# Conditional residual kernel: the adapters' first weights loaded before the ids are known, the order of its first turns changed

## The reference

```
x = x + einsum('bct,bcd->bdt', x, cond_weights[cond])        # per sample 64 x 64
x = x + einsum('bsi,boi->bso', x, adapter_weight[adapter])   # per sample 1024 x 1024
cond    = randint(0, 16, (128,));  adapter = randint(3, 8, (128,))
```

## Time and profile before

| | |
|---|---|
| median of three runs | 795.91 us |
| profiled execution | 799.4 us |
| its span, first to last instruction | 797.7 us |
| PE busy | 780.7 us, 98% |
| granted clock, mean | 0.997 |
| first z matmul starts | 24.88 us |
| slot 1 starts | 36.79 us |
| last PE work ends, by the chain of waits | 792.70 us |

### The profile page before, as it was taken

The page is one execution under the profiler, slowest core; times in us unless marked ns, Lnnn a source line. Parts: engine busy times, 40 slices in busy tenths (PEclk is TensorE's granted clock), DMA queues, the critical chain, the costliest instruction groups (busy, mean ns, idle before and its releaser), DMA issues.

```text
span 797.7 us, 19299 instructions
## 1 busy us (share of the span) xinstructions
PE 780.7 (98%) x3480; PEld 646.8 (81%) x3481; DVE 590.1 (74%) x707; ACT 455.9 (57%) x773; POOL 254.5 (32%) x158
## 2 busy tenths in 40 slices
PE   5999999999999999999999999999999999999997
PEld 4788888888888888888888888888888888888885
DVE  7777987788887567888876788887576756756764
ACT  3565666566556555765655566566554654555554
POOL 1444434243452212335431243452122122122110
PEclk9999999999999999999999999999999999999998
DMA  8345454444532334444333444532332233233133
GB/s 249 98 110 153 128 144 122 124 123 138 154 99 85 105 91 119 128 148 139 98 105 105 121 121 141 156 97 88 105 96 76 78 105 91 67 105 102 60 102 81
DMA packets 73956, 90.91 MB, mean 114 GB/s; under 512 B 13781, under 2 KB 64470, under 8 KB 73942
## 3 DMA queue, kind: packets, MB, share of 16 engines
q1 hardware_dynamic: 63654, 58.11, 24.2%
q10 hardware_dynamic: 10288, 32.65, 14.4%
HBM read 57.15 MB, written 33.55 MB: 114 GB/s over the span
## 4 chain that ended last, share of the span: by engine, by line
PE 97%; DMA 2%; DVE 0%; POOL 0%; issue 0%; SPq 0%; ACT 0%; POOLq 0%
PE z_ps L557 15%; PE z_ps L558 15%; PE first_ps L557 15%; PE first_ps L558 15%; PE z_ps L560 15%; PE first_ps L560 13%; PE y_ps L570 7%; DMA w_nat<-in_L_cond_weight_dram 2%; PE y_ps L538 0%; PE first_ps L538 0%; PE first_ps L641 0%; PE first_ps L639 0%; PE first_ps L638 0%; PE y_ps L652 0%; POOL w_nat L312 0%
## 5 line engine op out<-in xcount | busy, mean ns | idle before, releaser
L353 POOL TENSOR_TENSOR xt_lo<-x_turned,xt_hi 128x1024 fp32r<-128x1024 f32 x61 | 146.6, 2403 | 250.5 <-ACT xt_hi L699 246.5
L557 PE MATMUL z_ps<-w_hi,xt_hi 128*128 (+1 forms) x528 | 205.8, 390 | 0.0
L558 PE MATMUL z_ps<-w_lo,xt_hi 128*128 (+1 forms) x528 | 205.4, 389 | 0.0
L557 PE MATMUL first_ps<-w_hi,xt_hi 128*128 x520 | 202.4, 389 | 0.0
L558 PE MATMUL first_ps<-w_lo,xt_hi 128*128 x520 | 202.3, 389 | 0.0
L560 PE MATMUL z_ps<-w_hi,xt_lo 128*128 (+1 forms) x512 | 199.2, 389 | 0.0
L1005 DVE TENSOR_TENSOR y<-y_ps,y 64x512 f32<-64x512 f32 x252 | 173.2, 689 | 31.9 <-ACT y L715 26.0
L560 PE MATMUL first_ps<-w_hi,xt_lo 128*128 x472 | 183.6, 389 | 0.0
L715 ACT ACTIVATE y<-y_ps 64x512 f32<-64x512 f32 x252 | 149.1, 593 | 9.9 <-issue 2.0
L704 ACT ACTIVATE z_parts<-z_ps 64x512 fp32r<-64x512 f32 x132 | 78.4, 594 | 130.2 <-PE y_ps L570 92.8
L704 ACT ACTIVATE z_parts<-first_ps 64x512 fp32r<-64x512 f32 x130 | 77.2, 594 | 129.4 <-PE y_ps L570 102.8
(11 more groups left out here) (147 smaller groups left out, 387.6 us busy)
## 6 DMA issues: line engine op xcount, KB each, us to landing
x_in<-in_x_dram SPq DMA_DIRECT2D x536, 64.0 KB, 2.6
out_dram<-y ACTq DMA_DIRECT2D x124, 256.0 KB, 3.7
w_nat<-in_L_cond_weight_dram SPq DMA_DIRECT2D x128, 128.0 KB
w_nat<-in_L_cond_weight_dram SPq DMA_DIRECT2D x4, 512.0 KB, 8.1
y<-in_L_cond_weight_dram SPq DMA_DIRECT2D x2, 512.0 KB, 9.3
w_turned<-in_L_cond_weights_dram SPq DMA_DIRECT2D x2, 256.0 KB, 3.9
x_in<-in_x_dram SPq DMA_DIRECT2D x2, 256.0 KB, 5.6
x_turned<-in_L_cond_weight_dram SPq DMA_DIRECT2D x1, 512.0 KB, 6.9
```

The lines of the kernel that those rows point to most:

```text
L353: nc.gpsimd.tensor_tensor(xt_lo[h][:], x_turned[h][:], xt_hi[h][:].bitcast(F32), ALU.subtract).then_inc(xt_lo_made, 1)
L557: nc.tensor.matmul(to, xt_hi[h][:, t, :], whi, start=(t == 0), stop=False)
L558: mm = nc.tensor.matmul(to, xt_hi[h][:, t, :], wlo, start=False, stop=last and not pair)
```

## The change

1. Ids are reversed (7 - id) when the groups are sorted, so the group of id 7 comes first and the group of id 3 last. Its first five chunks are loaded before any id is known; if the first group is not id 7, they are loaded again.
2. The ids are no longer loaded one per partition; two small matmuls spread the clipped rows (`ids_spread`). PE runs 12 matmuls of 128x128 before them and 2 after, whose result nobody reads (`warm`).
3. Turn order: chunks 0 to 3, x of slot 0, chunks 4 to 7 (before: chunks 0, 1, x, 2 to 7). x of slot 0 is loaded with the samples' channels on alternate partitions. Two turns (chunks 6, 7) stand amid z's first half, after 3 and after 5 of its 8 tiles.
4. DVE's remainders are put between the table's small operations; the number of samples in slot 0 is known from the row of ids.
5. The condition matrices are loaded after the chunks. x of slot 1 is loaded half by SP and half by ACT, ACT between its rounding of chunk 6 and chunk 7. DVE turns x of slot 1 before it writes `slot_row`, and waits for `w0_lo_made` before that writing. SP reads `pair_count` after the first chunk load instead of before.
6. At the end, the wait for the store of y's buffer 1 moves behind the placing of W0.

```diff
-        TURN_ORDER = [0, 1, X0, 2, 3, 4, 5, 6, 7]
+        AHEAD_OF_IDS = 5
+        TURN_ORDER = [0, 1, 2, 3, X0, 4, 5, 6, 7]
-        LAST_TURNS = 1
-        TILES_FIRST = 3
+        WARMING, WARMING_ON = 12, 2
+        TURNS_WITHIN = (3, 5)
...
+            for c in range(AHEAD_OF_IDS):
+                sp.dma_start(first_nat[c], adapter_rows[((NAD - 1) * CHUNKS_PER_GROUP + c) * P:((NAD - 1) * CHUNKS_PER_GROUP + c + 1) * P, :]).then_inc(first_loaded[c], 16)
...
+            with sp.If(first_ad < NAD - 1):
+                for c in range(AHEAD_OF_IDS):
+                    sp.wait_ge(first_loaded[c], 16)
+                    load_first(c)
+            with sp.Else():
+
+                for c in range(AHEAD_OF_IDS):
+                    sp.sem_inc(first_loaded[c], 16)
+
+            sp.wait_ge(samples_made, 2)
...
+                sp.dma_start(x_in[0][k:P:2, :], x_rows[bass.ds(sample * C, C), :]).then_inc(x0_loaded, 16)
...
-            sp.wait_ge(table_moved, 16)
-            pairs_past = look_pairs_past(sp)
-            sp.wait_ge(table_ready, 1)
-            sp.wait_ge(groups_ready, 1)
-            sp.wait_ge(first_turned, NH * len(TURN_ORDER))
-            load_chunks(0)
-            load_chunks(1)
+            load_samples([look_early(sp, 2, field) for field in (SAMPLE_A, SAMPLE_B)], 0)
+
+            sp.wait_ge(first_turned, NH * len(TURN_ORDER))
+            sp.wait_ge(groups_ready, 1)
+            sp.wait_ge(table_ready, 1)
+            up_to, = look(sp, 1, CHUNKS)
+            load_chunks_between(0, up_to)
+            pairs_past = look_pairs_past(sp)
             slot(0, 1)
...
+            def warm(times):
+
+                for _ in range(times):
+                    nc.tensor.matmul(first_banks[2][0][:, 0:P], ones, ones, start=True, stop=True)
+
+            pe.wait_ge(consts_made, 3)
+            warm(WARMING)
             pe.wait_ge(consts_made, CONSTS)
+            pe.wait_ge(row_clipped, 1)
+            nc.tensor.matmul(ids_ps[:, 0:1], clipped_row, ones[0:1, 0:1], start=True, stop=True)
+            pe.wait_ge(row_clipped, 2)
+            nc.tensor.matmul(ids_ps[:, 1:2], cond_row, ones[0:1, 0:1], start=True, stop=True).then_inc(ids_spread, 1)
+            warm(WARMING_ON)
             pe.wait_ge(dve_step, MEMBER_STEP)
...
-            turn_first(0)
+            for i in range(TURNS + 1):
+                turn_first(i)
             pe.wait_ge(hot_made, 1)
...
-            for i in range(len(TURN_ORDER)):
+            for i in range(len(TURN_ORDER) - 1):
                 keep_first_hi(i)
+
+            act.wait_ge(table_made, 1)
+            load_sample(act, look_early(act, 1, SAMPLE_B), 1, 1)
+            keep_first_hi(len(TURN_ORDER) - 1)
             act.wait_ge(w0_with_1, 1)
             nc.scalar.activation(w0_all[:, :, 0], w0_nat, ACT.Copy).then_inc(w0_hi_made, 1)
             act.sem_inc(xt_hi_made, 1)
+            keep_z_hi(0, 0, 0)
             keep_xt_hi(1, 1)
-            keep_z_hi(0, 0, 0)
...
-            row_link(nc.vector.tensor_copy(ids_row, ids_row_i))
+            row_link(nc.vector.tensor_scalar(ids_row, ids_row_i, -1.0, float(NAD - 1), ALU.mult, ALU.add))
...
+            turn_x(0, 1)
+
+            dve.wait_ge(w0_lo_made, 1)
 
             dve.wait_ge(table_moved, 16)
...
             dve.wait_ge(table_ready, 1)
-            turn_x(0, 1)
-
-            dve.wait_ge(w0_lo_made, 1)
             turn_chunks(0)
```

More of the change, by code:

```diff
@@ L412, in _ @@
-            for c in range(2):
-                load_first(c)
-            sp.wait_ge(samples_made, 1)
-            _, first_samples = nc.values_load_multi_w_load_instructions(
-                first_samples_i[:], engines=[sp.engine], min_val=0, max_val=B - 1,
-                skip_runtime_bounds_check_because="the table is made on the chip, of clipped indices")
-            for k, sample in enumerate(first_samples):
-                sp.dma_start(x_in[0][k * C:(k + 1) * C, :], x_rows[bass.ds(sample * C, C), :]).then_inc(x0_loaded, 16)
@@ L421, in _ @@
-            for c in range(2, CHUNKS_PER_GROUP):
-                load_first(c)
-            sp.wait_ge(table_made, 1)
-            sp.dma_start(slot_row[:, 1:LOOKED_UP + 1, :], table_i[0:LOOKED_UP]).then_inc(table_moved, 16)
             def load_x(s, h):
                 load_samples(look(sp, s, SAMPLE_A, SAMPLE_B), h)
-            def load_early_x(s, h):
-                _, samples = nc.values_load_multi_w_load_instructions(
-                    table_i[s:s + 1, SAMPLE_A:SAMPLE_B + 1], engines=[sp.engine], min_val=0, max_val=B - 1,
-                    skip_runtime_bounds_check_because="the table is made on the chip, of clipped indices")
-                load_samples(samples, h)
@@ L446, in load_chunks, with load_chunks_between @@
             def load_chunks(s):
-                first, last = look(sp, s, CHUNKS_BEFORE, CHUNKS)
+                load_chunks_between(*look(sp, s, CHUNKS_BEFORE, CHUNKS))
+            def load_chunks_between(first, last):
                 with sp.If(last > first):
@@ L600, in _ @@
             nc.tensor.matmul(seconds_ps, hot[1], vals[:], start=True, stop=True).then_inc(gathered, 1)
[L602 removed]
+            for i in range(TURNS + 1, len(TURN_ORDER) - len(TURNS_WITHIN)):
                 turn_first(i)
[L605 removed]
+            pe.wait_ge(samples_made, 2)
             stores = look_first_stores(pe)
@@ L672, in _ @@
         def _(act):
-            with nc.allow_non_contiguous_dma(reason="one index per partition"):
-                act.dma_start(ids_i[:, 0:1], adapter_ids.rearrange("(b u) -> b u", u=1)).then_inc(ids_loaded, 16)
-                act.dma_start(ids_i[:, 1:2], cond_ids.rearrange("(b u) -> b u", u=1)).then_inc(ids_loaded, 16)
+            act.dma_start(cond_row_i, cond_ids.rearrange("(u b) -> u b", u=1)).then_inc(cond_row_loaded, 16)
             act.wait_ge(consts_made, CONSTS)
@@ L886, in _, with keep_x0_lo, keep @@
             row_linked()
-            nc.vector.tensor_scalar(first_samples_i[:], places[:], 2.0 * B, None, ALU.add).then_inc(samples_made, 1)
+            nc.vector.tensor_scalar(first_samples_i[:, 0:2], places[:], 2.0 * B, None, ALU.add).then_inc(samples_made, 1)
+            def keep_x0_lo(i):
+                def keep(samples, to):
+                    for n in range(NH):
+                        tiles = slice(n * TPB, (n + 1) * TPB)
+                        dve.wait_ge(first_hi_made, NH * i + n + 1)
+                        nc.vector.tensor_tensor(by_sample(to, tiles)[:, :, :, samples],
+                                                in_turns(first_banks[i % TURNS][n][:])[:, :, :, samples],
+                                                by_sample(xt_hi[0], tiles)[:, :, :, samples].bitcast(F32),
+                                                ALU.subtract).then_inc(first_lo_made, 1)
+                dve.wait_ge(samples_made, 2)
+                stores = look_first_stores(dve)
+                with dve.If(stores > 1):
+                    keep(slice(0, 2), xt_lo[0])
+                with dve.Else():
+                    keep(slice(1, 2), xt_hi[0])
             dve.wait_ge(counted, 1)
```

222 lines of the change are left out of this document (128 added, 94 removed).

## The result

The changed kernel takes 799.84 us (median of 6 runs, 798.55 to 800.18), the kernel before 795.89 beside it (795.38 to 796.55): a ratio of 1.0045, 95% interval 1.0035 to 1.0055. It is 3.95 us slower, and outside the forecast's range by 0.6 us. The profiled execution took 800.15 us with a span of 798.4, 0.3 us above its own median; that of before was 3.5 us above its median.

The account below looks back on a forecast made before the run. PE, busy 98% of the span, was taken to bound the kernel. SP's chunk clock leaves 0.15 us of the head's gain, the end costs 0.8: 795.91 + 0.65 = 796.6 us, range 793.6 to 799.2.

Parts of the forecast that it names:

- The head's steps: Head: z at 20.1 us, 4.8 earlier; `table_ready` at 31.8, 1.2 later; slot 1 at 35.0 against 36.79.
- The two stalls of PE: Head: PE stalls 1.6 us ahead of z's other half, waiting for chunk 7's remainder, then waits ahead of slot 1.
- The strided split of x: Slot 0, ACT and DVE: 0.645 at the least, taken; at most twice that, 1.3 us more before z.
- The first step that failed: Method: differences worked out within the profiled execution (799.4 us), then taken off the median, 795.91.
- The second step that failed: Last slot: one sample saves PE 3.63 us; its second half ends by ACT's and DVE's chain, so 1.81 are lost.
- The give-back of 1.0 at the end: End: one matmul fewer, PE starts at once, last store issued sooner with less ahead; 0.3 to 1.7 us together.
- SP's clock: Slot 4: chunk loads follow SP's issues; chunk 3 comes 1.05 us late of 1.2 spare, leaving 0.15 us gain.
- rival A: First group: SP's issues run quicker and do not bind, so slot 1's 1.8 us stay: 794.9; chance 0.17.
- Rival B: Head: ACT's issues hidden or short, table comes with the chunks, PE's work alone counts: 792.4 us; chance 0.13.
- Rival C: Head: PE loses its clock, ids or turns come late, Z at about 22: 798.5 us; chance 0.25.
- Z over 21: Rival C's mark: start of z (Z) later than 21 us; the forecast had 20.1.
- The swizzle: Load of x of slot 0: alternate partitions reach all ports, saving about 1 us of load, none of the sum.

Follow-up runs that it names:

- e_ascending: Changed kernel with ids and groups in ascending order again (early loads take adapter 3), table values clamped at zero: 797.54 us, 1.0017 of before.
- c_before: Control: the kernel before with only a clamp at zero on table values that engines read: 797.16 us, 1.0010 of before.
- e_reversed: Kernel before with only the groups reversed (7 - id), table values clamped at zero: 798.75 us, 1.0031 of before.
- c_after: Control: the changed kernel with only a clamp at zero on table values that engines read: 800.74 us, 1.0054 of before.
- v_best: Changed kernel, ascending, x of slot 0 consecutive, idle matmuls only in two waits, slot 1's x remainder before the table, ACT's reads before its loop: 794.97 us, 0.9986.
- e_end_reads: Changed kernel with ACT's table reads for the last slots moved ahead of its loop, table values clamped: 799.45 us, 1.0032 of before.
- v_reversed: v_best with ids and groups reversed as in the changed kernel: 797.06 us, 1.0010 of before.
- v_no_fill: v_best without its 2 and 4 idle matmuls in the waits: 795.68 us, 0.9994 of before.
- c_after_again: Changed kernel with only the clamp on table values, run and profiled once more: 800.65 us, 1.0054 of before.
- e_x_rows: Changed kernel with x of slot 0 on consecutive partitions, table values clamped: 800.61 us, 1.0054 of before; in a second run 799.87, 1.0048.
- e_nowarm: Changed kernel without its idle matmuls (0 and 0 in place of 12 and 2), table values clamped: 800.62 us, 1.0046 of before.
- e_xt_first: Changed kernel with POOL making slot 1's remainder of x before waiting for the table, table values clamped: 799.98 us, 1.0044 of before.
- e_fill: Changed kernel with x of slot 0 on consecutive partitions and 5 and 4 idle matmuls in two PE waits, table values clamped: 799.02 us, 1.0041 of before.
- e_spec_before: Kernel before with early loads of five chunks (adapter 3), condition matrices' loads moved behind the chunks, table values clamped: 799.11 us, 1.0036 of before.

## Why the prediction was wrong

**The head's steps held.** z at 20.1 (19.95), `table_ready` at 31.8 (31.33), slot 1 at 35.0 (35.52), SP's first chunk at 33.7 (34.12), chunk 7 behind ACT's issues: all within 0.6 us. The two stalls of PE did not: 1.6 us was forecast ahead of z's other half and came as 0.5; 0.75 ahead of slot 1, and came as 1.7. Their sum is right by luck. The strided split of x, taken at its lower bound, cost about two thirds of the way to its upper one: 2.1 us a pair instead of 1.1 on ACT.

Two steps failed, each by about 1.7 us. The numbers for each are worked out from single profiles, so they are estimates.

**The first step that failed: "I work differences out within the profiled execution and take them off 795.91".** The profiled execution was 3.5 us above the median, and the excess sat in the stretch that the change rewrites: slot 1 at 36.79, where an execution nearer the median has 33.4. A changed head that starts slot 1 at 35.5 is 1.3 us early against the one and 2 us late against the other. Before's head waits for its chunk loads, whose landing varies: between 15 us and z PE waited for 1.8, 1.7 and 0 us in its three profiles. The changed one waits for its own chain: 35.52, 35.71, 35.69. In time this shows as follows. e_ascending at its median (797.54) starts the last slot at 776.89. c_before's two profiles, moved to their medians, start it at 775.4 and 775.3. So the new head, with the slots behind it, loses 1.5 us, where the sum had a gain of 0.15. Against the profiled execution the forecast was 799.4 + 0.65 = 800.05, and the changed kernel's profiled execution took 800.15; even that is two errors which cancel, slot 1 early by 1.3 us instead of 0.15 and the rest longer by 2.0 instead of 0.8.

**The second step that failed: in the end's 0.8 us (0.1 to 1.5), that half of the one-sample slot's saving is kept, "1.81 of the 3.63 us are lost".** Nearly all of it was lost. From the start of the last slot to PE's last y row:

| | two samples last | one sample last |
|---|---|---|
| before, c_before; e_reversed | 14.56, 14.64 us | 14.53 us |
| e_ascending; changed kernel, c_after | 14.58 us | 14.33, 14.50 us |
| reads ahead: v_best; e_end_reads, v_reversed | 14.53 us | 12.78, 12.81 us |

With one sample PE's first half of the slot is 1.8 us shorter (16 instead of 24 matmuls), but ACT begins the next rounding 2.3 us behind its last store issue, by loop exit and table reads. It does so in before too (783.53, 2.31 behind its issue), where PE is hardly earlier: there ACT comes 0.1 to 0.3 us behind the moment that PE's y would allow, here 2.0. With the reads ahead of the loop 1.7 us come back, the 1.81 that the sum had counted on. The controls give the reversal 3.2 us in the changed kernel and 1.6 in before, against 0.8.

**The give-back of 1.0 at the end came**, and in part by another way. From PE's last y row to the end of the span it is 5.9 us in before and 5.3 to 5.4 in the two profiles of c_before, 4.3 in e_reversed, 4.1 to 4.3 in the changed kernel: 1.0 to 1.8. But e_ascending, v_best and v_no_fill, with two samples and the same pieces to store as before, have 4.2 to 4.3 as well: their last store lands 2.3 to 2.4 us after its issue instead of 3.5 to 4.0. So the changed kernel has this gain without the reversal, and nothing is left to set against the reversal's price, while in before the reversal brings it: about 1 us of the difference between 3.2 and 1.6. Why that store lands sooner was not tested.

**SP's clock (0.15 us of gain left) did not bind at slot 4.** SP issued eight loads of x in 3.83 us where before took 4.87 and 5.31, so its second chunk went out at 44.87, as early as before's (44.91). This is the mechanism of rival A. The forecast called itself wrong if PE had no wait in slots 1 to 5; it has some, but of 0.75 us instead of 1.6, and in slots 1 and 2. What binds there is POOL and DVE behind chunk 0's landing, and it differs from one execution to the next: slots 1 to 8 lost 0.75, 2.7 and 1.7 us in three profiles of the changed kernel, 0.0 to 1.5 in three of before.

**Rival B's sum**, with the turn and the hand-overs as costs, is -4.8 + 0.8 + 0.3 = -3.7 and its time 793.0, not 792.4. The forecast did not use it.

**Rival C** was right in part. z did not come late, so its mark (Z over 21) failed; but PE does lose its clock behind the waits that the changed head has: 0.83 to 0.85 over a 10 us stretch in seven of ten profiled executions of the changed kernel and its variants without filled waits (after, c_after_again, e_ascending, e_end_reads, e_x_rows and its second run, e_nowarm; not c_after, e_xt_first, v_no_fill), and in none of the three of before. At 10 to 20 us it costs little while z waits for the strided x (19.1 to 20.0 us with it, 19.7 and 19.9 without), and 1.6 us with consecutive rows (19.65 against 18.03). At 30 to 40 us slot 1 takes 13.5 us instead of 11.9, and 0.6 of it comes back in slot 2. The Trainium skill ("TensorE: Matmul & The Clock Gate", part 1) has it for the warm-up that the number of slow matmuls varies from run to run because the monitor runs freely. The traces agree on the varying: in before's three profiles the turns reach full pace at 18.8, 16.1 and about 14.5 us. Behind the waits it varies too: c_after shows no low stretch and c_after_again, the same code, shows two. That the monitor is the reason no run here shows.

**The swizzle.** Asked for at about 10 us, x landed in 2.9 to 3.2 us on alternate partitions (six profiles) and in 3.4, 4.0 and 3.5 on consecutive ones. The Trainium skill ("SBUF — State Buffer", the section on door 1) points the right way; the size is 0.2 to 1.1 us, and it bought a split that costs 0.9 us more.

**What stays open.** The intervals leave room: the 3.2 and 1.6 us of the reversal are good to about 1.3 and 1.1. How much of the loss in time is the clock's is argued and not shown. The mean clock of the timed runs is 0.9958 in c_after and 0.9973 in e_ascending, which would be worth 1.2 us; but within these kernels it does not go with the time: e_ascending took 797.4 to 797.9 us in its three runs at 1.000 and 797.4 and 798.7 in its two at 0.994; c_after_again took 800.43 at 0.998 and 800.65 and 800.31 at 0.994. In the kernel with consecutive rows it does: the second run of e_x_rows took 800.8 and 800.9 at 0.995 and 799.3 to 799.9 at 0.996 and 0.997.

## What to carry to other kernels

When the profiled execution is not at the median, find where its excess sits before taking a difference from it: if it is in the stretch that you change, the forecast can be off by as much as the excess, and two or three more profiles of the same kernel would tell. A step that is hidden beside long work (a loop's exit, table reads) comes to light when that work becomes shorter; list what the neighbours do there, and do not trust the name that a view gives to a wait when two engines come within 0.3 us of each other. And a start that a fixed chain sets is worth no more than the fastest usual start of the one that it replaces.

## What the runs showed of the hardware

- A copy or subtraction of 128x512 float32 from PSUM with its columns interleaved by two took 1.05 us a piece on ACT and 1.08 on DVE, against 0.55 and 0.65 with consecutive ones.
- A plain float32 matmul of 128 columns took 0.44 us (two records of 0.22) in the twelve at the start, and 0.26 in e_fill's five behind four quick turns.
- ACT spent 2.3 us between its last DMA issue in a loop and the first instruction behind the loop and two table reads (2.29 to 2.34 in 13 profiles), and 0.6 us with the reads ahead of the loop (e_end_reads, v_reversed).
- Where a stretch behind a wait was at 0.83 to 0.85 of the clock over 10 us, the slot in it took 13.5 us instead of 11.9 (e_x_rows, e_nowarm, c_after_again).
- Turns of eight 128-column transposes took 1.9 us in the first 18 us of e_spec_before, whose row for that stretch still has a granted clock of 1.00, and 1.07 behind it: the row of the clock does not show the slow start, the durations do.
- Early loads of five chunks, with the condition matrices' loads moved behind them, made the kernel before slower by 2 us (e_spec_before), though its profile starts z 1.2 and 2.4 us earlier than two of before's three.
